# Cross-attention normalised after PSUM: four heads share one reciprocal, spread by a selection matrix

## The reference

```python
def _L0_xattn_ref(x, context, Wq, Wk, Wv, Wo, bo):
    q = (x @ Wq).reshape(B, Sq, h, d).transpose(0, 2, 1, 3)
    k = (context @ Wk).reshape(B, -1, h, d).transpose(0, 2, 1, 3)
    v = (context @ Wv).reshape(B, -1, h, d).transpose(0, 2, 1, 3)
    scores = jnp.einsum('bhid,bhjd->bhij', q, k) * scale
    attn = jax.nn.softmax(scores, axis=-1)
    out = jnp.einsum('bhij,bhjd->bhid', attn, v)
    return out.transpose(0, 2, 1, 3).reshape(B, Sq, h * d) @ Wo + bo
x = x + jnp.tanh(g_xattn[0]) * _L0_xattn_ref(_layernorm(x, axis=-1), ctx_768, ...)
```

## Time and profile before

| | |
|---|---|
| median of 3 runs | 926.62 us (918.84 to 928.03) |
| profiled execution | 932.81 us, span 931.0 us |
| mean granted TensorE clock | 0.861 of full speed |
| PE busy | 764.6 us |
| DVE busy | 634.9 us |
| ACT busy | 353.3 us |
| POOL busy | 299.8 us |

### The profile page before, as it was taken

The page is one execution under the profiler, slowest core; times in us unless marked ns, Lnnn a source line. Parts: engine busy times, 40 slices in busy tenths (PEclk is TensorE's granted clock), DMA queues, the critical chain, the costliest instruction groups (busy, mean ns, idle before and its releaser), DMA issues.

```text
span 931.0 us, 13102 instructions
## 1 busy us (share of the span) xinstructions
PE 764.6 (82%) x5120; PEld 406.8 (44%) x5120; DVE 634.9 (68%) x1216; ACT 353.3 (38%) x444; POOL 299.8 (32%) x422
## 2 busy tenths in 40 slices
PE   4679798988999779987899799978898876786583
PEld 2355564644564245532464245534463433242231
DVE  0615577898655787678787988788556786964724
ACT  1324226214535234532545244632534244263060
POOL 5043442532244014332164135322244120333033
PEclk9879799998789788996899899996889778688587
DMA  5310300400303013030403023030503043023000
GB/s 146 76 35 15 69 10 10 101 11 6 74 15 57 11 54 77 12 57 6 113 18 60 9 66 71 21 42 8 128 1 54 1 108 78 2 68 57 2 1 12
DMA packets 64734, 40.95 MB, mean 44 GB/s; under 512 B 4912, under 2 KB 62776, under 8 KB 64664
## 3 DMA queue, kind: packets, MB, share of 16 engines
q1 hardware_dynamic: 64672, 40.12, 19.8%
HBM read 22.99 MB, written 17.10 MB: 43 GB/s over the span
## 4 chain that ended last, share of the span: by engine, by line
PE 52%; DVE 22%; DMA 12%; SPq 6%; ACT 4%; issue 2%; POOL 2%; POOLq 0%; DVEq 0%
PE psum L564 12%; DVE mx8B L903 12%; PE psum L651 8%; PE psum L571 6%; DMA q8B<-q_dB 6%; PE psum L607 5%; PE psum L639 3%; DVE mxA L826 3%; PE psum L545 3%; PE psum L555 2%; DMA qA<-mrow_d 2%; DMA k8F<-k_dF 2%; PE psum L614 2%; PE psum L620 2%; PE psum L550 1%
## 5 line engine op out<-in xcount | busy, mean ns | idle before, releaser
L903 DVE TENSOR_REDUCE mx8B<-psum 128x2 f32<-128x1024 f32 x128 | 149.9, 1214 | 42.0 <-PE psum L620 41.8
L564 PE MATMUL psum<-qA,cTX 97*128 97x256 f32 x512 | 146.7, 438 | 15.9 <-DMA qA<-mrow_d 12.8
L717 ACT ACTIVATE probB<-psum 128x1024 f32<-128x1024 f32 x128 | 125.7, 1026 | 53.9 <-PE psum L639 53.5
L951 POOL TENSOR_TENSOR half<-probX 128x512 f32<-128x512 f32 x64 | 81.5, 1274 | 165.7 <-ACT probX L704 164.9
L564 PEld LDWEIGHTS psum<-qA,cTX 97*128 97x128 f32 x512 | 106.1, 216 | 46.0 <-issue 21.8
L704 ACT ACTIVATE probX<-psum 128x1024 f32<-128x1024 f32 x64 | 65.6, 1024 | 158.4 <-PE psum L564 158.4
L620 PE MATMUL psum<-k8B,q8B 48*128 48x512 bf16 x256 | 60.8, 476 | 58.5 <-DVE mx8B L903 27.6
L717 ACT ACTIVATE probF<-psum 128x1024 f32<-128x1024 f32 x64 | 64.5, 1025 | 105.6 <-PE psum L639 104.0
L898 DVE TENSOR_REDUCE mx8F<-psum 128x4 f32<-128x1024 f32 x64 | 77.0, 1220 | 35.8 <-PE psum L614 35.7
L834 DVE RECIPROCAL rden<-psum 128x256 f32<-128x256 f32 x32 | 56.2, 1757 | 55.7 <-PE psum L575 55.6
L826 DVE TENSOR_REDUCE mxA<-psum 128x2 f32<-128x1024 f32 x64 | 76.9, 1216 | 13.5 <-PE psum L555 13.3
(11 more groups left out here) (191 smaller groups left out, 1129.7 us busy)
## 6 DMA issues: line engine op xcount, KB each, us to landing
k8B<-k_dK SPq DMA_DIRECT2D x16, 384.0 KB, 6.1
k_dK<-partsK SPq DMA_DIRECT2D x8, 384.0 KB, 4.0
q8F<-q_dF SPq DMA_DIRECT2D x16, 192.0 KB, 4.5
k8F<-k_dF SPq DMA_DIRECT2D x16, 192.0 KB, 4.9
q8B<-q_dB SPq DMA_DIRECT2D x16, 192.0 KB, 7.4
k_dK<-partsK SPq DMA_DIRECT2D x8, 256.0 KB, 4.0
cTX<-in_ctxT SPq DMA_DIRECT2D x8, 192.0 KB, 2.4
cTK<-in_ctxT SPq DMA_DIRECT2D x8, 192.0 KB, 2.5
```

The source lines that it names most:

```text
L564: last = mm(ps[:, c * SEQ:(c + 1) * SEQ], cT["X"][:, c * P:(c + 1) * P], qA[:, k, :], start=True, stop=True)
L717: nc.scalar.activation(prob[s][(units * b + k) % SLOTS[s]][:], ps, ACT.Exp, scale=float(D8) ** -0.5).then_inc(done["ACT"], 1)
L903: nc.vector.tensor_reduce(mx8[s][:, t, 2 * p:2 * p + 2], ps.rearrange("p (i n) -> p i n", i=2), AX.X, ALU.max, negate=True).then_inc(drain ...
L951: link("X", engine.tensor_tensor(half[:], p[:, 0:2 * SEQ], p[:, 2 * SEQ:], ALU.add))
```

## The change

X's `pv` holds only the value matmuls, and ACT copies the result undivided into `oTX`. Twice per sequence, a new fill `sm` adds four heads' `psum_k` over the partitions, each into 32 rows of one bank (32 columns of `ones` per head, four side by side), and DVE takes one reciprocal of 128x256 for the four heads. A new fill `bc` multiplies `rden` by `spread`, a constant 128x2x128 matrix of zeros and ones, in two full-size matmuls, so that each head's reciprocal stands on the head's 64 rows; DVE multiplies 128x512 of `oTX` by it in place. `out` waits for the second `bc`. POOL's `psum_k` buffers are freed by `sm`, four at a time, in place of `pv`. The planner's durations and waits follow, so the order of all jobs is worked out anew.

```diff
--- before.py
+++ after.py
@@ -81,13 +81,16 @@
     for k in range(XH):
         g = XH * b + k - SLOTS["X"]
         freed = "PE", "X", "pv", g // XH, g % XH // 2
-        p.fill("ACT", 1, "X", "e", b, k, 2.0, 1.03, [("SP", "X", "mr", b, 0), ("ACT", "X", "qp", b, k // 4)], [freed])
-        p.job("POOL", "X", "e", b, k, 2.0, ("ACT", "X", "e", b, k), freed)
+        p.fill("ACT", 1, "X", "e", b, k, 2.0, 1.03, [("SP", "X", "mr", b, 0), ("ACT", "X", "qp", b, k // 4)],
+               [freed, ("POOL", "X", "e", g // XH, g % XH)])
+        p.job("POOL", "X", "e", b, k, 2.0, ("ACT", "X", "e", b, k), ("PE", "X", "sm", g // XH, g % XH // 4))
     for k in range(XH // 2):
-        p.fill("DVE", 0, "X", "pv", b, k, 2.7, 2.2,
-               [("ACT", "X", "e", b, 2 * k + 1), ("POOL", "X", "e", b, 2 * k + 1), ("ACT", "X", "vp", b, 1)],
-               [("PE", "X", "out", b - 1, 0)])
-    p.fill("DVE", 0, "X", "out", b, 0, 2.0, .49, [("DVE", "X", "pv", b, 3)],
+        p.fill("ACT", 0, "X", "pv", b, k, 1.8, .39,
+               [("ACT", "X", "e", b, 2 * k + 1), ("ACT", "X", "vp", b, 1)], [("PE", "X", "out", b - 1, 0)])
+    for k in range(2):
+        p.fill("DVE", 0, "X", "sm", b, k, .6, 1.76, [("POOL", "X", "e", b, 4 * k + 3)], [("PE", "X", "bc", b - 1 + k, 1 - k)])
+        p.fill("DVE", 0, "X", "bc", b, k, .95, .69, [("DVE", "X", "sm", b, k)], [("ACT", "X", "pv", b, 2 * k + 1)])
+    p.fill("DVE", 0, "X", "out", b, 0, 2.0, .49, [("DVE", "X", "bc", b, 1)],
            [("POOL", "X", "xb", b, 0), ("POOL", "F", "fin", b - 1, 0)])
 
 
@@ -301,7 +304,8 @@
 
         ident = sb("ident", [P, P])
         iota = sb("iota", [P, NE])
-        ones = sb("ones", [P, XD])
+        ones = sb("ones", [P, 32])
+        spread = sb("spread", [P, 2, P])
         wqk = sb("wqk", [P, XH, CD])
         wvx = sb("wvx", [CD, XH * XD])
         wox = sb("wox", [P, XH // 2, P])
@@ -416,7 +420,7 @@
 
         block = ctx.enter_context(nc.Block())
 
-        loads = [(wo8[:], a["wo8"]), (iota[:], a["iota"]), (wox[:], a["wox"]),
+        loads = [(wo8[:], a["wo8"]), (iota[:], a["iota"]), (wox[:], a["wox"]), (spread[:], a["spread"]),
                  (be[:], a["be"]), (bg[:], a["bg"].rearrange("(o n) -> o n", o=1).broadcast_to([P, NE]))]
         for s in "FB":
             loads += [(wq8[s][:], a["wq8" + s]), (wk8[s][:], a["wk8" + s]), (wv8[s][:], a["wv8" + s]),
@@ -568,13 +572,19 @@
                     for c in range(KV // P):
                         for i in range(2):
                             h = 2 * k + i
-                            mm(ps[64 * i:64 * i + 64, 0:SEQ], vX[:, c, h * XD:(h + 1) * XD],
+                            last = mm(ps[64 * i:64 * i + 64, 0:SEQ], vX[:, c, h * XD:(h + 1) * XD],
                                prob[s][h % SLOTS[s]][:, c * SEQ:(c + 1) * SEQ], start=(c == 0), stop=(c == KV // P - 1))
-                    pe.wait_ge(*up_to("X", "psum", b, 2 * k + 2))
-                    for i in range(2):
-                        last = mm(ps[64 * i:64 * i + 64, SEQ:2 * SEQ], ones[:], psum_k[(2 * k + i) % 4][:], start=True, stop=True)
+                elif name == "sm":
+                    pe.wait_ge(*up_to("X", "psum", b, 4 * k + 4))
+                    for j in range(4):
+                        last = mm(ps[32 * j:32 * j + 32, 0:SEQ], ones[:], psum_k[j][:], start=True, stop=True, tile_position=(0, 32 * j))
+                elif name == "bc":
+                    pe.wait_ge(*is_done("X", "sm", b, k))
+                    pe.wait_ge(w_loaded, W_LOADS)
+                    for j in range(2):
+                        last = mm(ps[:, j * SEQ:(j + 1) * SEQ], spread[:, j, :], rden[:], start=True, stop=True)
                 elif name == "out":
-                    pe.wait_ge(*is_done("X", "pv", b, XH // 2 - 1))
+                    pe.wait_ge(*is_done("X", "bc", b, 1))
                     pe.wait_ge(w_loaded, W_LOADS)
                     for t in range(QT):
                         for j in range(XH // 2):
@@ -701,6 +711,7 @@
                 elif name == "e":
                     g = XH * b + k - SLOTS["X"]
                     act.wait_ge(*is_full("X", "pv", g // XH, g % XH // 2))
+                    act.wait_ge(*up_to("X", "psum", g // XH, g % XH + 1))
                     nc.scalar.activation(prob[s][k % SLOTS[s]][:], ps, ACT.Exp, scale=float(XD) ** -0.5).then_inc(done["ACT"], 1)
                 elif name in ("qk", "kk"):
                     act.wait_ge(*after(s, "sw", b - 1))
@@ -715,6 +726,9 @@
                     g = units * b + k - SLOTS[s]
                     act.wait_ge(*is_full(s, "pv8", g // units, g % units // (KEYS[s] // P)))
                     nc.scalar.activation(prob[s][(units * b + k) % SLOTS[s]][:], ps, ACT.Exp, scale=float(D8) ** -0.5).then_inc(done["ACT"], 1)
+                elif name == "pv":
+                    act.wait_ge(*is_full("X", "out", b - 1))
+                    nc.scalar.activation(oTX[:, k, :], ps[:, 0:SEQ], ACT.Copy).then_inc(done["ACT"], 1)
                 elif name == "pv8":
                     act.wait_ge(*is_full(s, "oT", b - 1, 1))
                     nc.scalar.activation(oU[s][:, k, :], ps[:, 0:SEQ], ACT.Copy).then_inc(done["ACT"], 1)
@@ -828,11 +842,13 @@
                 elif name == "mT":
                     dve.wait_ge(*after("X", "mw", b - 1))
                     nc.vector.tensor_copy(mrow[:], ps[0:XH, 0:SEQ]).then_inc(drained, 1)
-                elif name == "pv":
-                    dve.wait_ge(*is_full("X", "out", b - 1))
-                    dve.wait_ge(*(is_done("X", "pv", b, k - 1) if k else is_done("X", "pv", b - 1, XH // 2 - 1)))
-                    link(s, nc.vector.reciprocal(rden[:], ps[:, SEQ:2 * SEQ]))
-                    nc.vector.tensor_tensor(oTX[:, k, :], ps[:, 0:SEQ], rden[:], ALU.mult).then_inc(drained, 1)
+                elif name == "sm":
+                    dve.wait_ge(*is_full("X", "bc", b - 1 + k, 1 - k))
+                    nc.vector.reciprocal(rden[:], ps[:, 0:SEQ]).then_inc(drained, 1)
+                elif name == "bc":
+                    dve.wait_ge(*is_done("X", "pv", b, 2 * k + 1))
+                    nc.vector.tensor_tensor(oTX[:, 2 * k:2 * k + 2, :], oTX[:, 2 * k:2 * k + 2, :],
+                                            ps.rearrange("p (j n) -> p j n", j=2), ALU.mult).then_inc(drained, 1)
                 elif name in ("out", "out8"):
                     dve.wait_ge(*after(s, "xb", b))
                     dve.wait_ge(*after("F" if s == "X" else "C", "fin", b - 1))
@@ -945,7 +961,7 @@
                 elif name == "e":
                     pool.wait_ge(*is_done("X", "e", b, k))
                     g = XH * b + k - 4
-                    pool.wait_ge(*is_full("X", "pv", g // XH, g % XH // 2))
+                    pool.wait_ge(*is_full("X", "sm", g // XH, g % XH // 4))
                     pool.wait_ge(*up_to("X", "psum", b, k))
                     p = prob[s][k % SLOTS[s]]
                     link("X", engine.tensor_tensor(half[:], p[:, 0:2 * SEQ], p[:, 2 * SEQ:], ALU.add))
@@ -989,6 +1005,7 @@
     arrays = {
         "x": g["x"], "ctxT": g["ctx_768"].transpose(0, 2, 1), "g_xattn": g["g_xattn"], "g_ffn": g["g_ffn"],
         "ident": np.eye(P, dtype=np.float32),
+        "spread": np.kron(np.eye(4, dtype=np.float32), np.outer(np.eye(1, 32), np.ones(XD))).reshape(P, 2, P).astype(np.float32),
         "iota": np.tile(np.arange(NE, dtype=np.float32), (P, 1)),
         "wqT": g["L0_xattn_Wq"].reshape(P, XH, XD).transpose(2, 1, 0),
         "wkT": g["L0_xattn_Wk"].reshape(CD, XH, XD).transpose(2, 1, 0),
```

## The result

| | before | after |
|---|---|---|
| median, same chip | 927.33 us (918.84 to 934.35) | 957.08 us (948.64 to 964.97) |
| profiled execution | 932.81 us | 964.97 us, span 963.2 us |
| mean granted TensorE clock | 0.861 | 0.853 |

The ratio is 1.0322, with a 95% interval of 1.0199 to 1.0445: slower, by about 30 us, where 932 us was forecast with a range of 914 to 946. The ratio is that of the fast runs (medians 956.5 and 926.6 us), and both profiled executions are slower than their medians, after by 0.8% and before by 0.6%.

The account below looks back on a forecast made before the run. No engine was taken to bound the whole; PE was full in X's stretches. PE +12.6, less 2.4 and 3.1 hidden, less 2.0 for DVE, plus 0.5 for loading: +5.6 on 926.6, so 932 us, range 914 to 946.

Follow-up runs that it names:

- a_out: Changed kernel with only X's `out` of sequences 4, 5 and 6 put ahead of B's first maxima on PE and DVE; 964.96 us, ratio 1.0437.
- a_sp: Changed kernel with only SP's order put back, X's maxima read `mr` ahead of F's reload `sr` in sequences 2 to 7; 948.15 us, ratio 1.0235.
- a_mx: Changed kernel with only F's first maxima put behind the heads of X on PE and DVE, SP's order left changed; 965.71 us, ratio 1.041.
- a_oldorder: Changed kernel with every shared job in the order of the kernel before, only `sm`, `bc` and ACT's copies placed by the planner; 968.11 us, ratio 1.0373.
- a_dep_again: Changed kernel, plan waits added: F's reload after next X's maxima read, F's first maxima after X's head 3; repeat run, 912.93 us, ratio 0.9882 to kernel before.
- b_dep_again: Kernel before, plan waits added: F's reload after next X's maxima read, F's first maxima after X's head 3; repeat run, 909.78 us, ratio 0.9859 to kernel before.

## What to carry to other kernels

Where a program works out the order of all jobs, an edit has two prices: its own work, and the order that comes out. Read the order of the queues in the changed kernel before believing a sum over instructions, above all which small transfer stands behind which large one on the way to a full engine. To judge an edit, pin the doubtful places with explicit waits and compare both kernels under them: here that showed the edit to be worth nothing that can be measured, and the two waits, with the order that follows from them, to be worth 1.4 to 2.1% in the kernel before.

A stall seen in the chain is not worth its length when it is taken away (`a_out`: 5 us visible, none won), and of two blockades in series each is worth little alone (`a_sp` 1.0235, `a_mx` 1.041, together 0.9972).

## What the hardware showed that was not expected

- A small DMA behind large ones: `mr` lands 1.80 us after its issue when it goes ahead of F's reloads (554.32 in before) and 4.93 us behind F's four reloads (457.60 in before). On top of the 2.6 us in which SP issues the four, it landed 3.1 us later.
- The first head after a wait does not tell the whole cost. A wait of 1.18 us (before, sequence 5) left all eight heads at full clock, and one of 2.94 us (`a_oldorder`, sequence 5) had the first head at 3.75 us. In between stand waits of 2.77 us (before, sequence 7) and 2.04 us (after, sequence 4): their first heads took 2.01 and 1.99 us, but three later heads of each sequence ran at or near the 1.2 GHz level, in before at once:

```profile
664.10 2.01 PE L564 MATMUL psum<-qA,cTX 97*128 97x256 f32 x8 [2.77 <-DMA qA<-mrow_d]
...
667.44 3.78 PE L564 MATMUL psum<-qA,cTX 97*128 97x256 f32 x8
```

What PE had done before differs between these, so they are sightings and no threshold.
- The mean granted clock differs between orders of nearly the same work: 0.861 in before, 0.853 in after, 0.841 in `a_oldorder`, 0.877 in both `a_dep_again` and `b_dep_again`. One kernel by itself moves as well: the executions of before went from 0.850 to 0.878, so only the distance between `a_oldorder` and the last two is clear of that.
